# Turning softmax blocks through DRAM: their transfers ahead of weight loads on SyncE's queue, and one batch more of them

## The reference

```python
xl      = layernorm(x)                                    # (8, 256, 512): batch, D, T
theta_x = einsum('ld,bdt->btl', theta_w, ctx) + theta_b   # L = 128
phi_x   = einsum('ld,bdt->blt', phi_w, xl) + phi_b
p       = softmax(theta_x @ phi_x, axis=-1)               # (8, 512, 512)
g_x     = einsum('ld,bdt->btl', g_w, xl) + g_b
t_x     = einsum('bts,bsl->blt', p, g_x)
h       = relu((t_x - mean) * rsqrt(var + 1e-5) * gamma + beta)   # over all of (L, T)
x       = x + tanh(g_xattn) * (out_w @ h + out_b + ctx)
# feed-forward on layernorm(x): three linear layers, activations quantised to 8 bit
# by row, weights to -1, 0, 1 by their mean absolute value
x       = x + tanh(g_ffn) * bitlinear(silu(bitlinear(xl, w1)) * bitlinear(xl, w2), w3)
```

## Time and profile before

| | |
|---|---|
| median of 3 runs | 303.91 us (301.97, 303.91, 303.98) |
| the profiled execution | 302.16 us, of which the span is 300.4 us |
| busy, share of the span | TensorE 97%, VectorE 80%, GpSimd 66%, ScalarE 65% |
| granted TensorE clock, mean | 0.999 |
| moved by DMA | 42.23 MB, 141 GB/s over the span |
| chain that ended last | TensorE 75%, DMA 10%, VectorE 4%, ScalarE 4% |

### The profile page before, as it was taken

How to read it: one execution, slowest core, us unless ns; L and a number is a source line. 1 busy time by engine, 2 the same in 40 slices (tenths; PEclk the granted TensorE clock), 3 DMA queues, 4 the chain that set the end, 5 groups by cost and what they waited for, 6 DMA issues and landing times.

```text
span 300.4 us, 4393 instructions
## 1 busy us (share of the span) xinstructions
PE 291.4 (97%) x1310; PEld 155.7 (52%) x1310; DVE 240.0 (80%) x539; ACT 195.7 (65%) x319; POOL 198.4 (66%) x302
## 2 busy tenths in 40 slices
PE   8999979999899999999999999999999999999996
PEld 6765736574566565644444444444444444444444
DVE  3797976989598797799988788887986896877872
ACT  1487985989789988799954736455465547345720
POOL 3363597868665767765988778576786786665610
PEclk9999999999999999999999999999999999999999
DMA  7999956546967201010324565154324363551355
GB/s 256 393 420 413 406 170 235 159 122 217 308 209 265 70 0 37 0 37 2 70 42 80 92 114 132 29 113 105 71 72 106 70 91 87 107 138 21 87 99 180
DMA packets 56535, 42.23 MB, mean 141 GB/s; under 512 B 43456, under 2 KB 46656, under 8 KB 55488
## 3 DMA queue, kind: packets, MB, share of 16 engines
q1 hardware_dynamic: 56224, 41.69, 48.1%
q10 hardware_dynamic: 288, 0.27, 0.3%
HBM read 24.65 MB, written 6.82 MB: 105 GB/s over the span
## 4 chain that ended last, share of the span: by engine, by line
PE 75%; DMA 10%; DVE 4%; ACT 4%; issue 3%; SPq 2%; POOL 1%; POOLq 0%; DVEq 0%; ACTq 0%
PE bank L1238 37%; PE bank L1256 14%; PE bank L1182 7%; DMA spill<-blocks 5%; PE bank L1154 4%; PE bank L1199 3%; PE bank L1169 2%; PE bank L1118 2%; DMA placed<-spill 2%; PE bank L1141 2%; DMA x<-x_dram 2%; PE bank L1269 1%; PE bank L1131 1%; DMA probT<-prob 1%; SPq L258 1%
## 5 line engine op out<-in xcount | busy, mean ns | idle before, releaser
L1238 PE MATMUL bank<-wq,stage 128*128 128x512 bf16 x512 | 113.3, 379 | 0.0
L1238 PEld LDWEIGHTS bank<-wq,stage 128*128 128x128 bf16 x512 | 50.1, 98 | 61.5 <-issue 2.3
L872 DVE SCALAR_TENSOR_TENSOR stage<-bank,s,stage 128x512 f32<-128x512 f32 x64 | 47.6, 745 | 22.5 <-PE bank L1238 18.6
L615 ACT ACTIVATE xn<-stage 128x1024 f32<-128x1024 f32 x31 | 32.8, 1057 | 46.1 <-DVE stage L872 46.1
L607 ACT ACTIVATE stage<-bank,s 128x512 f32<-128x512 f32 x64 | 43.2, 681 | 16.4 <-PE bank L1238 14.3
L1256 PE MATMUL bank<-wq,prob 128*128 128x512 bf16 x224 | 50.5, 379 | 0.0
L467 POOL TENSOR_SCALAR stage<-stage,hsc 128x1024 f32<-128x1024 f32 x30 | 33.3, 1120 | 20.6 <-DVE hsc L903 20.6
L877 DVE TENSOR_REDUCE m<-stage 128x1 f32<-128x1024 f32 x31 | 37.7, 1216 | 0.8
L1256 PEld LDWEIGHTS bank<-wq,prob 128*128 128x128 bf16 x224 | 21.9, 98 | 26.4
L1154 PE MATMUL bank<-ph,th 128*128 128x512 f32 x96 | 34.4, 471 | 0.0
L473 POOL TENSOR_SCALAR prob<-stage 128x1024 bf16<-128x1024 f32 x30 | 30.9, 1044 | 0.0
(11 more groups left out here) (122 smaller groups left out, 461.1 us busy)
## 6 DMA issues: line engine op xcount, KB each, us to landing
stage<-w1t_dram SPq DMA_DIRECT2D x4, 1024.0 KB, 11.4
stage<-w2t_dram SPq DMA_DIRECT2D x4, 1024.0 KB, 14.7
stage<-w3t_dram SPq DMA_DIRECT2D x4, 1024.0 KB, 6.7
x<-x_dram SPq DMA_DIRECT2D x7, 512.0 KB, 5.6
c_sb<-ctx_in_dram SPq DMA_DIRECT2D x7, 512.0 KB, 7.6
out_dram<-stage SPq DMA_DIRECT2D x14, 256.0 KB, 2.4
spill<-blocks SPq DMA_DIRECT2D x5, 512.0 KB, 7.7
placed<-spill SPq DMA_DIRECT2D x20, 128.0 KB, 2.8
```

Source lines behind the costliest of these rows:

```text
L615: A.activation(junk, h_sb[t % 2][:, half * HF:(half + 1) * HF], ACT.Square, accum_out=ssq[:, half:half + 1]).then_inc(sq_done, 1)
L872: V.scalar_tensor_tensor(h_sb[k][:, c * 512:(c + 1) * 512], up_banks(n)[1][:, :], s12[:, u % 2, 1, k:k + 1], sil[n % 3], ALU.mult, ALU.mul ...
L1238: last = mm(bank[:, :], turned[:, row:row + P], wq[:, at:at + 512], start=q == 0, stop=q == KI - 1)
```

## The change

It has two parts. In SyncE's queue the two last chunks of w2 come behind `move_blocks(1)`, w3's chunk 0 behind `move_blocks(3)` and the others of w3 each by one place among contexts and moves. And `by_blocks` holds for batch 6 as well. Its chunks 2 and 3 are then turned by VectorE and moved by SyncE (`move_blocks(6)`, in front of `turn_x(0)`), ScalarE normalises two of its chunks, and its two products on `placed` stand behind the last scores of batch 7. `turn_no` counts TensorE's turns anew. GpSimd's `quant_h` waits for `blocks_ready` too, as it overwrites `prob`.

```diff
         def by_blocks(i):
-            return 1 <= i <= B - 3
+            return 1 <= i <= B - 2
 
         def turn_no(i, c):
-            return c + (2 * i + 2 if by_blocks(i) else 0 if i == 0 else 2 * (B - 3) + 4 * (i - (B - 3)))
+            return min(c, 2) + 2 * i + 2 if by_blocks(i) else c if i == 0 else c + 4 + 2 * (B - 2)
...
             load_weight(1, 1)
-            load_weight(1, 2)
-            load_weight(1, 3)
             load_c(3)
             load_x(4)
             move_blocks(1)
+            load_weight(1, 2)
+            load_weight(1, 3)
             load_x(5)
             load_c(4)
             move_blocks(2)
             load_x(6)
             load_x(7)
-            load_weight(2, 0)
             load_c(5)
             move_blocks(3)
+            load_weight(2, 0)
+            load_c(6)
             load_weight(2, 1)
+            move_blocks(4)
             load_weight(2, 2)
-            load_c(6)
-            move_blocks(4)
+            load_c(7)
             load_weight(2, 3)
-            load_c(7)
             move_blocks(5)
+            move_blocks(6)
...
                 if t < 2:
                     pool.wait_ge(pT_done, turn_no(B - 2 + t, TC))
+                    pool.wait_ge(blocks_ready, 2 * (B - 2))
...
                 scores(i, 3)
                 if whole:
                     values(i - 1, 3)
+                elif i == B - 1:
+                    values(i - 1, 2)
+                    values(i - 1, 3)
```

## The result

The changed kernel takes 298.30 us (median of 4 runs, 298.23 to 298.47). The kernel before took 303.25 beside it (four runs, 301.97 to 303.98). The ratio of the runs is 0.984, 95% interval 0.980 to 0.988: faster, by more than the 1% that can be told from no change. The 5.0 us between these medians flatter the change, because two of the four runs of the kernel before took 303.91 and 303.98, more than any of its 41 runs since. The profiled execution took 298.30 us with a span of 296.5, against 302.16 and 300.4: 3.86 us less.

A forecast was written before the change was run, and what follows sets the result against it. TensorE, busy 97% of the span, was taken to bound the kernel. On the profiled scale 302.16 - 1.9 - 2.0 + 0.1 = 298.4 us; against the median 300.1, so the middle, 299.3 us, was named, range 297.2 to 302.4.

The forecast's parts named there:

- What bounds the kernel: TensorE, busy 97% of the span; gains lie only in its gaps before 121 us.
- Batch 1, gain 1.9: Iteration 3: w2's last chunks behind the blocks remove the placed gap, 2.48 us, less 0.6 given back.
- The part given back before line 1207: Iteration 3: TensorE waits for VectorE's mean of batch 1, not before 48.9 instead of 48.3, losing 0.6 us.
- Batch 3, gain 2.0: Iteration 5: spill issued at 60.2 behind context 5 alone, so the placed gap goes whole, 2.0 us.
- the slack of over 5 us: Iteration 5: batch 3's blocks land at 67.0, TensorE wants them at 72.7.
- The moved loads, zero: Later w2 and w3 chunks, contexts and x loads on SyncE's queue cost nothing; w3's chunk 2 zero to 0.3.
- Batch 6, loss 0.1: Iteration 7: VectorE's block turns delay hn, relu stops TensorE's lead; loss 0.1 us, between -0.9 and +1.3.
- The rule against it: Batch 6's turns: skill says transpose 128 x 128 on TensorE; 0.87 us there against 1.23 us on VectorE.
- TensorE's lead: Iteration 7: TensorE 0.8 us ahead before out_proj(5,0), but gets nothing as it waits for relu(5).
- The sum: Whole kernel, on the profiled execution's scale: 302.16 - 1.9 - 2.0 + 0.1 = 298.4 us.
- The named 299.3: Whole kernel: forecast median 299.3 us, the middle between 298.4 (profiled run) and 300.1 (shown median).
- the middle between two levels of runs: Single runs of the kernel before: two near 302, two near 304; next level unknown, so the middle named.

The follow-up runs named there:

- e3: Only w2's chunks 2 and 3 moved behind the blocks of batch 1, against the kernel before: 300.53 us, ratio 0.997.
- e2: Batch 6 by blocks alone, SyncE's queue in its old order, against the kernel before: 302.22 us, ratio 1.001.
- e1: SyncE's new queue order alone, batch 6 turned on TensorE as before, against the kernel before: 298.06 us, ratio 0.987.
- e4: Only w3's chunks in their new order, w2's as before, against the kernel before: 299.55 us, ratio 0.992.
- w1: Changed kernel with w2's chunk 3 one move later, behind the loads of batch 2: 306.99 us, ratio 1.017 to the kernel before.
- r3: Changed kernel with relu(5) before chunk 2's exponential, center(1) behind batch 7's normalisations, GpSimd's normalisation before w3's first two roundings: 297.52 us, again 297.76.
- n1: New queue order and the three moves of r3, but batch 6 turned on TensorE as in the kernel before: 297.97 us.
- r4: r3 with VectorE's steps on hn for batch 5 (tx_dev, tx_gamma) ahead of prep_scale(0): 298.00 us.

## Why the prediction was right

*What bounds the kernel.* Right. TensorE's account by iteration explains all 3.86 us, and nothing behind 121 us changed.

*Batch 1, gain 1.9.* Measured 2.15 in the two profiles that I compared. The spill took 2.6 us and its loads were issued from 36.06, as worked out (35.9). The part given back before line 1207 was 0.24 us, not 0.6. Line 1207 started at 48.53, not at 48.9, because GpSimd had the normalisation of batch 2 done 0.4 us earlier. In the first set the same part gained 1.1 us by the medians (e3) and 1.2 by theta's spacing (e2 against e1), since the gap there was 1.31: how long a transfer in a full queue takes is the least certain number of this sum.

*Batch 3, gain 2.0.* Measured 2.03, and 2.1 us by e4 alone. The spill took 3.8 us, not 2.6, which the slack of over 5 us covered.

*The moved loads, zero.* Right. No step of ScalarE waited for a weight. w3's chunk 2 was issued at 79.17, near the 79.8 of the sum. w1 shows that the concern was real: one chunk, one move later, costs 8.6 us.

*Batch 6, loss 0.1.* The mechanism held: VectorE late, TensorE ahead and stopped by relu. The size was 0.26 to 0.29 us (changed kernel, e2). 0.2 of it is a step that I put on the wrong engine. I started the block turns when ScalarE's normalisations end, 4.38 us behind theta. They started 102.43 - 97.85 = 4.58 us behind it, released by GpSimd's, which `prep_root(0)` holds in that iteration. The same 0.2 us is missing from TensorE's lead: I had 0.8 us, and r3, where neither relu nor GpSimd stops it, shows 0.6.

*The rule against it.* The advice of the Trainium skill, "VectorE: DVE Perf Modes", section "Rules for kernel authors", TensorE for 128 x 128, would have the kernel without this part. In the change as made that is right by 0.3 us in the trace. With relu moved the trace says the opposite, by 0.5 us (r3 against n1), which the times don't show. It isn't the cost of the transpose alone that decides, but whose time is late.

*The sum.* 298.4 against the 298.30 of the profiled execution. That it is this near is luck in part: batch 1 won 0.25 us more than the sum had and batch 6 lost 0.19 more, and the two nearly cancel. So do two parts that the sum had no term for, 0.10 us less in iterations 4 and 6 and 0.13 us by which theta(3) started later. The named 299.3 was 1.0 us too high: the failing step is the middle between two levels of runs. Later runs show no two levels. The kernel before took 301.20 to 302.43 us in 40 of 41 runs on three chips, with medians of 301.6 to 301.9, and once 303.53, at a clock of 0.994. The three shown runs held two near 304. What made those two longer isn't known.

## What to carry to other kernels

A small transfer that an engine will wait for belongs ahead of a large one that nobody needs yet, even on a queue with bandwidth to spare. Work out each moved load's landing against the step that reads it, since a chunk a few us late costs its lateness and then the clock.

Work taken off the busiest engine counts only up to its next wait. Before moving work to another engine, look at what stands directly behind the freed stretch. Here it was one short instruction queued behind an exponential that waited for VectorE.

From one profiled execution, give the sum on that execution's own scale.

## What the runs showed that I had not expected

- A VectorE instruction that reads two tiles in SBUF was held up until a GpSimd instruction on large SBUF tiles that was already running had ended. r4's first addition started 0.18 us into line 434, took 1.40 us instead of 0.68, and ended 0.54 us behind it. The 223 other additions in the 14 traces, none of which started over such an instruction, took 0.68 to 0.69 us. The step on `hn` (807) shows it in every trace, here the changed kernel's:

```profile
113.30 0.74 DVE L807 SCALAR_TENSOR_TENSOR hn<-hn,tsc,pc 128x512 f32<-128x512 f32 x1
...
122.97 1.18 DVE L807 SCALAR_TENSOR_TENSOR hn<-hn,tsc,pc 128x512 f32<-128x512 f32 x1
...
122.50 1.12 POOL L402 TENSOR_SCALAR stage<-stage,winv 128x1024 f32<-128x1024 f32 x1
```

  It takes 0.74 us when GpSimd's instruction has at most 0.13 us left, 1.10 with 0.57 left, 1.18 with 0.64 left and 1.54 with 1.01 left (r4): in the last three cases it ends 0.54 us behind GpSimd's instruction. `add_out` (812), with one operand in PSUM, takes 0.74 us even with 0.99 left. The Trainium skill, "SBUF — State Buffer", section "Terms", says that VectorE and GpSimd share a port pair, which one of them holds for a whole instruction while the other is blocked. The traces agree for the instructions with two tiles in SBUF, and `add_out` shows no blocking.
- One wait of 1.44 us on the first context took theta(3) 2.3 us later than in e1: 1.4 by the wait, and 0.9 in phi(0), when the granted clock of the first two stages was 0.92 and 0.88 as means (e3). After a 5.65 us wait a stage of 5 us was granted 0.50, and that cost another 2.8 us (w1).
- A 512 KB store to DRAM took 2.6 us on an empty queue and up to 9.2 us behind loads that were still under way (batch 4 of the kernel before). For batch 1, with the same queue before it, it took 7.7 us in the profile before and 6.8 in two later ones, both of one chip (e2, e4).
